# The last nine units of a two-stage graph network in another order

## What is computed

```python
h = relu(layernorm(x))
x = x + L0(h, adj)      # h@W, scores, mask, softmax, keep the top 16, aggregate, elu
h = relu(layernorm(x))
x = x + L1(h, adj)      # three layers l = 0, 1, 2:
#   s    = leaky(h@wi[l] + (h@wj[l]).T + b[l]), masked by adj + identity
#   y1   = h + softmax(s) @ h ;   h1 = layernorm(y1) * g1[l] + beta1[l]
#   ff   = gelu(h1 @ W1[l] + b1[l]) @ W2[l] + b2[l]        # 256 -> 1024 -> 256
#   h    = layernorm(h1 + ff) * g2[l] + beta2[l]
```

## Time and profile before

| | us |
|---|---|
| median of three runs | 2841.56 |
| span of the profiled execution | 2840.5 |
| what lies around the span (median less span) | 1.1 |
| TensorE busy in the span | 2719.1 (96%) |
| ScalarE, VectorE, GpSimd busy | 2326.9, 2293.8, 2080.0 |

### The profile page before, as it was taken

How to read it: one execution, slowest core, us unless ns; L and a number is a source line. 1 busy time by engine, 2 the same in 40 slices (tenths; PEclk the granted TensorE clock), 3 DMA queues, 4 the chain that set the end, 5 groups by cost and what they waited for, 6 DMA issues and landing times.

```text
span 2840.5 us, 55392 instructions
## 1 busy us (share of the span) xinstructions
PE 2719.1 (96%) x17764; PEld 2449.2 (86%) x17764; DVE 2293.8 (81%) x7766; ACT 2326.9 (82%) x4806; POOL 2080.0 (73%) x2217
## 2 busy tenths in 40 slices
PE   4698999999999999999999999999999999999995
PEld 4578988999999998998899899999899999888884
DVE  6777888888888888888888888888888888887542
ACT  4577988888888888888888888888888888888763
POOL 0355777877777787787787777778777777877774
PEclk8798999999999999999999999999999999999997
DMA  5000010111011011101101110110111011010001
GB/s 182 25 27 27 29 33 11 32 35 35 27 34 35 9 34 35 35 27 35 35 9 35 35 35 27 35 34 9 35 35 34 27 35 27 19 25 20 11 10 15
DMA packets 96322, 88.63 MB, mean 31 GB/s; under 512 B 9120, under 2 KB 94368, under 8 KB 96032
## 3 DMA queue, kind: packets, MB, share of 16 engines
q1 hardware_dynamic: 79136, 68.32, 7.8%
q0 software_dynamic: 16896, 16.78, 4.6%
HBM read 47.34 MB, written 37.75 MB: 30 GB/s over the span
## 4 chain that ended last, share of the span: by engine, by line
PE 80%; POOL 5%; issue 5%; DVE 4%; ACT 3%; DMA 2%; POOLq 0%; SPq 0%; ACTq 0%; DVEq 0%
PE ps_ff L3065 11%; PE ps_mm L3042 11%; PE ps_mm L3044 11%; PE ps_mm L3043 10%; PE ps_ff L3066 10%; PE ps_ff L3067 10%; PE ps_ag L3100 5%; PE ps_ht L3112 3%; PE ps L3164 2%; DMA out<-H 2%; POOL a_lo L506 2%; PE ps_s L3088 1%; PE ps_s L3078 1%; PE ps L3177 1%; PE ps L3178 1%
## 5 line engine op out<-in xcount | busy, mean ns | idle before, releaser
L3065 PE MATMUL ps_ff<-w_hi,a_hi 128*128 128x256 f32 x3072 | 892.0, 290 | 10.1 <-POOL a_lo L506 5.3
L506 POOL TENSOR_TENSOR a_lo<-A,a_hi 128x512 fp32r<-128x512 f32 x384 | 524.3, 1366 | 486.7 <-ACT a_hi L1077 486.4
L3066 PE MATMUL ps_ff<-w_lo,a_hi 128*128 128x256 f32 x3072 | 855.6, 279 | 0.0
L3067 PE MATMUL ps_ff<-w_hi,a_lo 128*128 128x256 f32 x3072 | 855.0, 278 | 0.0
L1069 ACT ACTIVATE A<-ps_mm,b_col 128x512 f32<-128x512 f32 x768 | 517.3, 685 | 251.7 <-PE ps_ff L3067 147.8
L3042 PE MATMUL ps_mm<-ht_hi,w_hi 128*128 128x512 f32 x1536 | 627.0, 408 | 3.7 <-DVE ht_lo L2327 2.8
L3065 PEld LDWEIGHTS ps_ff<-w_hi,a_hi 128*128 128x128 f32 x3072 | 578.2, 188 | 45.7 <-issue 11.7
L3044 PE MATMUL ps_mm<-ht_lo,w_hi 128*128 128x512 f32 x1536 | 606.5, 395 | 0.0
L3043 PE MATMUL ps_mm<-ht_hi,w_lo 128*128 128x512 f32 x1536 | 604.6, 394 | 0.0
L3066 PEld LDWEIGHTS ps_ff<-w_lo,a_hi 128*128 128x128 f32 x3072 | 579.0, 188 | 12.5
L3067 PEld LDWEIGHTS ps_ff<-w_hi,a_lo 128*128 128x128 f32 x3072 | 579.2, 189 | 0.0
(11 more groups left out here) (120 smaller groups left out, 5315.2 us busy)
## 6 DMA issues: line engine op xcount, KB each, us to landing
xr<-in_x SPq DMA_DIRECT2D x32, 512.0 KB, 4.2
out<-x SPq DMA_DIRECT2D x32, 512.0 KB, 4.8
out<-H POOLq DMA_DIRECT2D x32, 512.0 KB, 6.2
mask_in<-mask_park SPq DMA_DIRECT2D x96, 128.0 KB, 4.1
adj_sb<-in_adj SPq DMA_DIRECT2D x32, 256.0 KB, 4.4
mask_park<-mask_out SPq DMA_DIRECT2D x32, 128.0 KB, 4.0
X<-in_L_gnn_W SPq DMA_DIRECT2D x3, 1024.0 KB, 5.2
H<-in_L_gnn_W SPq DMA_DIRECT2D x3, 1024.0 KB, 7.1
```

The source lines that it names most:

```text
L506: pool.tensor_tensor(a_lo[:, at], A[:, at], a_hi[:, at].bitcast(F32), ALU.subtract).then_inc(s["a_lo_gpsimd"], 1)
L3065: pe.matmul(out_g, a_hi[:, at, cols], w2_hi[:, l, m], start=first, stop=False, skip_group_check=True)
L3066: pe.matmul(out_g, a_hi[:, at, cols], w2_lo[:, l, m], start=False, stop=False, skip_group_check=True)
L3067: last = pe.matmul(out_g, a_lo[:, at, cols], w2_hi[:, l, m], start=False, stop=final, skip_group_check=True)
```

## The change

The last nine units get another order, and `closing` of all five engines (SyncE, GpSimd, ScalarE, VectorE, TensorE) is written out anew for it. `opening` and `iteration` are the same. Every call of before is there once, with the same operands: each engine's list is a permutation. The first call that differs is, on TensorE, at 2332.9 us of the trace of before. No instruction is added or removed; the counts that the semaphores wait for follow `UNITS`.

```diff
 UNITS = sorted(((k, l) for k in range(NG) for l in range(L)), key=lambda u: L * u[0] + (L + 1) * u[1])
+TAIL = [(-2, 0), (-3, 1), (-1, 0), (-4, 2), (-2, 1), (-1, 1), (-3, 2), (-2, 2), (-1, 2)]
+UNITS[len(UNITS) - len(TAIL):] = [(NG + k, l) for k, l in TAIL]
```

More of the change, by code:

```diff
@@ new lines, in closing @@
+                r_norm(NG - 1)
+                gelu(NG - 2, 0, 0)
+                a_high(NG - 2, 0, 0)
+                gelu(NG - 2, 0, 1)
+                gelu(NG - 2, 0, 2)
+                h_norm(NG - 3, 1)
+                a_high(NG - 2, 0, 1)
+                a_high(NG - 2, 0, 2)
+                leaky(NG - 1, 0)
+                gelu(NG - 2, 0, 3)
+                a_high(NG - 2, 0, 3)
+                gelu(NG - 2, 0, 4)
+                a_high(NG - 2, 0, 4)
+                exps(NG - 1, 0)
@@ L1872, in closing @@
+                gelu(NG - 2, 0, 5)
+                ht_high(NG - 3, 1, 0)
+                a_high(NG - 2, 0, 5)
+                p_copy(NG - 1, 0)
+                y_norm(NG - 5, 2)
+                gelu(NG - 2, 0, 6)
+                gelu(NG - 2, 0, 7)
+                ht_high(NG - 3, 1, 1)
+                a_high(NG - 2, 0, 6)
                 leaky(NG - 4, 2)
-                a_high(NG - 5, 2, 7)
-                ht_high(NG - 2, 0, 1)
-                h_norm(NG - 3, 1)
+                a_high(NG - 2, 0, 7)
@@ L1969, in closing @@
                 a_high(NG - 1, 0, 7)
+                gelu(NG - 4, 2, 0)
+                a_high(NG - 4, 2, 0)
+                h_norm(NG - 2, 1)
+                gelu(NG - 4, 2, 1)
+                ht_high(NG - 2, 1, 0)
+                a_high(NG - 4, 2, 1)
+                gelu(NG - 4, 2, 2)
+                a_high(NG - 4, 2, 2)
+                gelu(NG - 4, 2, 3)
+                y_norm(NG - 1, 0)
+                gelu(NG - 4, 2, 4)
+                a_high(NG - 4, 2, 3)
+                gelu(NG - 4, 2, 5)
@@ L1970, in closing @@
+                a_high(NG - 4, 2, 4)
+                ht_high(NG - 2, 1, 1)
+                a_high(NG - 4, 2, 5)
+                gelu(NG - 4, 2, 6)
+                gelu(NG - 4, 2, 7)
+                a_high(NG - 4, 2, 6)
                 gelu(NG - 2, 1, 0)
+                a_high(NG - 4, 2, 7)
                 a_high(NG - 2, 1, 0)
-                h_norm(NG - 3, 2)
+                leaky(NG - 1, 1)
                 gelu(NG - 2, 1, 1)
+                exps(NG - 1, 1)
+                a_high(NG - 2, 1, 1)
@@ L1974, in closing @@
                 gelu(NG - 2, 1, 2)
-                a_high(NG - 2, 1, 1)
+                p_copy(NG - 1, 1)
+                gelu(NG - 2, 1, 3)
                 a_high(NG - 2, 1, 2)
-                gelu(NG - 2, 1, 3)
-                y_norm(NG - 1, 0)
-                ht_high(NG - 3, 2, 0)
+                y_norm(NG - 4, 2)
                 a_high(NG - 2, 1, 3)
                 gelu(NG - 2, 1, 4)
+                leaky(NG - 3, 2)
+                a_high(NG - 2, 1, 4)
+                exps(NG - 3, 2)
@@ L2006, in closing @@
-                gelu(NG - 3, 2, 6)
-                gelu(NG - 3, 2, 7)
-                a_high(NG - 3, 2, 6)
-                leaky(NG - 2, 2)
-                a_high(NG - 3, 2, 7)
-                h_norm(NG - 1, 1)
-                exps(NG - 2, 2)
-                ht_high(NG - 1, 1, 0)
-                p_copy(NG - 2, 2)
                 ht_high(NG - 1, 1, 1)
```

1326 lines of the change are left out of this document (645 added, 681 removed).

## The result

The kernel after took 2853.27 us as a median of 6 runs (2849.27 to 2853.67), the kernel before beside it 2841.77 (6 runs, 2840.77 to 2844.69). The ratio is 1.0035, interval [1.0023, 1.0046]: 0.35% slower, some 10 us, by more than the 0.2% that the prediction took for its bound. The forecast was +3.0 us and "no change" the likeliest case (0.62, against 0.28 for slower); its sign was right and its size less than a third. The profiled execution took 2850.94 us with a span of 2848.9, 8.4 longer than the one of before. It is one of the two shorter ones of the six: the four others took 2853.19 to 2853.67, so the profile shows some 2.3 us less than the median.

What follows compares the result with a forecast made beforehand. TensorE's work was taken as the bound, its idle time as the difference. A loss of 0.6 us ahead of the end of mm2(-3,2,7) and 2.4 behind it made 3.0: 2841.56 + 3.0 = 2844.5 us, range 2834 to 2852.

Steps and rivals of the forecast that it cites:

- A: The end of mm2(-3,2,7) on TensorE; in before turn_h(-1,1,0) starts there, at 2724.08, with 116.4 us left.
- The second fall of the clock: Between A and mm1(-2,2,0): a rival in which the clock falls again and it shows, 2847.3 us, chance 0.10.
- Rival (a): Layers of the last groups cover one another, a_low(-2,2,0) isn't late, stalls ahead of A shrink: 2836.6 us, chance 0.14.
- Its own term: Behind A: node_scores(-1,2) on VectorE, up to turn_sj(-1,2), priced at 4.0 us.
- the count of what was moved ahead of A: Feed-forward of (-1,1), its two turn_h, and turn_p and both agg of (-2,2), already done at A: 24.5 us.
- the difference of the times is the difference of the idle times: On TensorE: work is the same in both lists, so idle time, plus what the clock takes, sets the change.
- The two places at which I expected waits: Ahead of A on TensorE: 0.6 us around the attention of (-3,2), some 2.0 at mm2(-3,2,5).
- small misfits between list and chip: Ahead of A: the rest of TensorE's idle time in the new list, 2.3 us, bounds 0 and 5.
- the steady rate: Ahead of A: TensorE idle at 4.75 / 2032 over some 415 us, 1.0 us.
- Rival (b): ScalarE becomes the bound in (-2,1); pairs of exps in (-2,0) and (-2,1) lose 4.5 us each: 2850.1 us, chance 0.22.
- The DMAs of SyncE's list: Mask loads stand many calls ahead of their scores_mask: nothing counted; a late load would cost its own lateness.
- The forecast's own range: 2840 to 2849 us for the whole kernel, around the forecast of 2844.5, chance 0.54.

Runs made afterwards that it cites:

- e6: The kernel after, but every call that started before 2410 us in the trace of before stands in the old order: ratio to before 1.0022.
- e12: The kernel after with the old order of calls up to 2410 us and filler matmuls in the two holes: ratio to before 1.0016.
- e9: The kernel before with a_low(-2,2,4) moved from GpSimd to VectorE, ahead of node_scores: 2844.0 us, one run.
- e7: The kernel after with filler matmuls in both holes and GpSimd's a_low(-2,2,0) right behind y_bias(-3,2,1), ahead of add_out(-3): 2856.2 us, one run.
- e3: The kernel after with filler matmuls in the holes ahead of the feed-forwards of (-2,2) and (-1,2): ratio to before 1.0026.
- e2: Calls that started before 2540 us in the trace of after in the new order, the rest as in the kernel before: ratio to before 1.0036.
- e10: The kernel before with filler matmuls in the hole of (-1,2) alone, GpSimd's list as before: ratio 1.0000.

## Why the prediction was too small

**What it had right.** The mechanisms behind A came in the order and nearly at the times of the sum: turn_h(-2,2,0) at A + 3.2 (3.1), waiting for ScalarE; mm1(-2,2,0) at 8.6 (8.2); mm2(-2,2,0) at 17.0 (16.7), waiting for GpSimd and hiding the clock; turn_sj(-1,2) at 28.9 (28.0); turn_p at 35.6 (34.1); mm1(-1,2,0) at 52.1 (50.5), so that the hole stayed, 16.6 us from turn_p (16.4); the end of the span at 96.0 (94.3). The second fall of the clock came. Rival (a) is wrong: GpSimd was late at mm2(-2,2,0), the starts of (-2,2) and (-1,2) stayed uncovered, and the calls ahead of A lost more, not less.

**Behind A: three terms were a little too small.** The forecast loss was 2.4 us, measured 4.3. Two of the three have to do with GpSimd and VectorE meeting. (1) y_norm(-3,2) began at A + 5.2 and not 5.0, and add_out was issued at A + 12.9 and not 12.7; mm2(-2,2,0) came 0.3 us late. The two a_low at 2767.92 take 3.54 us and not 2.6, with VectorE's a_low(-2,2,1), 2.06 us and not 0.69, beside them, but y_scale(-1,1,1) ahead of them began 0.5 us before add_out had ended, which makes up for the first. (2) turn_sj came 0.9 us late. 0.2 of this come from (1), as h_scale waits for the DMA; the two h_scale, 2772.02 to 2775.01, take 3.0 and not 2.6 (VectorE's a_low(-2,2,3) runs beside the second), and y_bias needs another 0.17 to start. Its own term, 4.0 us from y_bias on, held: one instruction of node_scores met GpSimd here as in before, which is the 1.51 us of the earlier trace rows that I had read as part of its wait. (3) The last one, the small tensor_scalar at 2781.73, met GpSimd too, 1.15 us where it takes 0.23. leaky waits for it and came 1.2 us after turn_sj, in before 0.7; mask, max and a_low(-2,2,7) follow on VectorE, mm2(-2,2,7) waited 0.31 for the last, and turn_p came 6.7 us after turn_sj and not 6.1. The 0.9 of (2), the 0.6 of (3) and 0.2 in the hole make 1.7 of the 1.9 missing. The rest is the count of what was moved ahead of A, 24.9 instead of 24.5.

**Ahead of A: the step that failed.** It reads "the difference of the times is the difference of the idle times", and it forecast 5.9 us idle against 5.3. Idle time came to 6.3, and still 4.4 us were lost. Busy rows of TensorE overlap, so short slips don't show as idle; in lists where every call is a little late, most of the loss is in them. The bounds of the term "small misfits between list and chip", 0 and 5, were drawn for idle time as well and left this out. The two places at which I expected waits were wrong too: mm2(-3,2,5) waited 0.14 us and not 2.0, and 4.72 of the 6.3 us idle lay between 2331 and 2500, which the prediction took at the steady rate and a share of the misfits. The cover there was named, VectorE at 140.42 of 168.00 us; it was busy for 145.64 of 169.00 in after, and mm2(-6,1,7) waited for it. ScalarE, 149.93 us and not 146.34, has less room still, and the prediction gave the new table loads no term there.

**Rival (b)** gave the time almost exactly (2850.1), and it is not what happened: the longest wait of TensorE for ScalarE anywhere between 2331 and A was 0.4 us, and all of them together 1.0 (0.4 in before). What ScalarE costs through a late a_high, and so a late a_low, these waits don't show. The DMAs of SyncE's list, counted at nothing, cost nothing that the waits show. The range, 2834 to 2852, holds the profiled execution and ends 1.3 us below the median of the runs; 2841.8 x 1.0035 is 2851.7. The forecast's own range, 2840 to 2849, holds neither. That the wide one does is luck: its upper end was there for (b).

**What stays open.** Of the 4.4 us ahead of A e6 removes 1.5 and shows that the order of the calls up to 2410 sets these (e12, with the same order, lost 17.6). The 2.9 others are the balance of slips over the next 120 calls, 4.9 us more than before, and what is won back later; no experiment names the cause of either. That the pulled-forward stage 0 fills VectorE there is argued from its busy time, not shown; the four table loads more on ScalarE are as good a candidate. Whether the wait of mm2(-5,0,7) is what makes four of the six executions 2.3 us longer than the profiled one is open too, as they have no profile.

## What to carry to other kernels

Compare two orders of the same work by the time from each call of the bounding engine to the next, against the median of its kind: idle time in the profile showed 1.0 of 4.4 us here. Before a hidden cost is removed (a low clock, a late transfer), look for what stands right behind it: fillers alone gave 0 us, the wait that the moved a_low avoids was there only with them, and both together gave 3.4. And where a unit is to start earlier, the work that feeds it has to be spread out earlier as well, which costs in a part of the schedule that looks untouched.

## What the runs showed of the hardware

- An instruction of VectorE that met one of GpSimd took 1.47 to 1.51 us instead of 0.41 (the reduction of two inputs in node_scores), 1.15 instead of 0.23 (a small tensor_scalar). node_scores took 3.1 us with none caught (e9), 4.2 with one (before), 5.1 with one and the tensor_scalar (after), 7.4 with four (e7).
- A stall of 1.9 to 2.7 us among the feed-forwards can be followed by 3.4 us at the lower clock, and need not be. In e3 a stall of 1.89 us ended at 2349.44 and the clock was at 0.50 from 2350.6 to 2354.0; in e2 one of 1.86 us ended at 2550.08, in e10 one of 2.69 at 2810.38 and in e12 one of 2.67 at 2770.99, and 3.4 us at 0.50 followed each. Behind the same wait of mm2(-5,0,7) as in e3, 1.89 us, the clock stayed at 1.00 in e7 (2347.61) and e2 (2349.82), and behind 2.69 us in e3 itself (2775.16). The stretch in e3, where 12 matmuls take 3.4 us:

```profile
2350.60:2354.00 3.40, 3.40 (x12) 2.71 (x11) 2.43 (x6) 3.37 (x11) 2.42 (x2) 0.50 0.03 9
```

- add_out on GpSimd's queue, 512 KB, took 6.2 us from its issue to the release of h_scale in before (2795.03 to 2801.22), after (2765.81 to 2772.02) and e10 (2799.80 to 2806.05), and 6.0 in e7 (2769.39 to 2775.36).
